# Layer 1 feed-forward: fetched expert results are added at another pace, from eight buffers instead of four

## The reference, cut to what matters

```python
x += sum over k of weight[t, k] * expert[e(t, k)](row[t])     # K = 4 of 32 experts, width 176
x += sigmoid(row @ w_shared_gate) * shared(row)                # width 704
shared(row) = (silu(row @ sw_gate) * (row @ sw_up)) @ sw_down
```

## Time and profile before

| what | us |
|---|---|
| median of 3 runs | 1801.31 |
| lowest and highest | 1800.06, 1802.41 |
| the profiled execution's own time | 1804.75 |
| its span, first to last instruction | 1802.7 |
| the end of layer 1's feed-forward, first shared down matmul to the last | 799.5 to 921.9 |
| the end of layer 2's feed-forward, to the closed statistics | 1348.6 to 1402.8 |

### The profile page before, as it was taken

One profiled execution on the slowest core, in us unless ns is written; L12 is line 12 of the kernel. 1 busy time (PEld: TensorE's weight loads), 2 busy tenths in 40 slices (PEclk: granted clock), 3 DMA queues, 4 the chain that ended last, 5 costly groups with the idle time before them and its releaser, 6 DMA issues. The chain is left out here.

```text
span 1802.7 us, 30396 instructions
## 1 busy us (share of the span) xinstructions
PE 1430.4 (79%) x8275; PEld 909.8 (50%) x8291; DVE 1149.8 (64%) x2546; ACT 754.5 (42%) x2273; POOL 595.2 (33%) x576
## 2 busy tenths in 40 slices
PE   4999993567589588997779999876883699975994
PEld 2565651345444253763346666553651466653552
DVE  3788887788578775324448999844335688844224
ACT  2766663344420032320027777521320588831321
POOL 2111100778477214335611111013436101002662
PEclk9999997898899678998879999957997799966997
DMA  7000000000010120962210001212433100411224
GB/s 251 10 6 9 9 4 1 1 0 0 13 35 0 52 91 29 305 213 80 87 31 10 12 9 62 87 56 56 122 102 87 36 24 23 154 52 33 82 81 154
DMA packets 73877, 111.35 MB, mean 62 GB/s; under 512 B 10381, under 2 KB 53200, under 8 KB 73296
## 3 DMA queue, kind: packets, MB, share of 16 engines
q1 hardware_dynamic: 61520, 77.99, 13.1%
q0 software_dynamic: 12288, 32.53, 6.5%
HBM read 87.41 MB, written 24.12 MB: 62 GB/s over the span
## 5 line engine op out<-in xcount | busy, mean ns | idle before, releaser
L523 ACT ACTIVATE l0a_prob<-l0a_ps_s,l0a_neg_max 128x128 f32<-128x128 f32 x512 | 141.0, 422 | 77.8 <-DVE l0a_neg_max L398 77.8
L523 ACT ACTIVATE l2a_prob<-l2a_ps_s,l2a_neg_max 128x128 f32<-128x128 f32 x512 | 141.0, 425 | 55.4 <-DVE l2a_neg_max L398 55.4
L878 ACT ACTIVATE l3a_prob<-l3a_ps_s,l3a_neg_max 128x256 f32<-128x256 f32 x256 | 104.5, 482 | 30.6 <-DVE l3a_neg_max L801 29.2
L398 DVE TENSOR_REDUCE l0a_neg_max<-l0a_ps_s 128x4 f32<-128x512 f32 x128 | 81.9, 684 | 38.0 <-PE l0a_ps_s L616 37.9
L369 POOL TENSOR_TENSOR l2a_k_head<-l2a_kT,head_of_row 128x512 f32<-128x512 f32 x32 | 32.6, 1041 | 178.7 <-ACT l2a_kT L504 178.7
L398 DVE TENSOR_REDUCE l2a_neg_max<-l2a_ps_s 128x4 f32<-128x512 f32 x128 | 82.1, 683 | 13.5 <-PE l2a_ps_s L616 13.4
L801 DVE TENSOR_REDUCE l3a_neg_max<-l3a_ps_s 128x2 f32<-128x512 f32 x128 | 84.2, 682 | 8.3 <-PE l3a_ps_s L929 8.0
L178 POOL TENSOR_TENSOR ln_rstd<-ln_var_eps,minus_half 128x16 f32<-128x16 f32 x8 | 23.4, 2921 | 196.3 <-POOLq L149 130.4
L1515 PE MATMUL l1a_ps_y<-l1a_kv,l1a_tap 128*128 128x512 f32 x192 | 84.2, 601 | 3.7 <-POOL l1a_kv L1487 3.7
L406 DVE COPY l2a_probT<-l2a_ps_t 128x512 f32<-128x512 f32 x128 | 82.0, 682 | 4.7 <-PE l2a_ps_t L625 4.6
L406 DVE COPY l0a_probT<-l0a_ps_t 128x512 f32<-128x512 f32 x128 | 82.1, 684 | 3.2 <-PE l0a_ps_t L625 3.1
(11 more groups left out here) (453 smaller groups left out, 3645.8 us busy)
## 6 DMA issues: line engine op xcount, KB each, us to landing
l1f_w_gu<-in_l1f_w_gu SPq DMA_DIRECT2D x32, 352.0 KB
expert_results<-l2f_y_sb SPq DMA_DIRECT2D x48, 128.0 KB
l1f_w_d<-in_l1f_w_d SPq DMA_DIRECT2D x32, 176.0 KB
expert_results<-l1f_y_sb SPq DMA_DIRECT2D x32, 128.0 KB
l2f_w_gu_all<-in_l2f_w_gu SPq DMA_DIRECT2D x1, 4096.0 KB, 13.7
l3f_w_gu_all<-in_l3f_w_gu SPq DMA_DIRECT2D x1, 4096.0 KB, 15.2
l3f_got<-expert_results SPq DMA_DIRECT2D x16, 256.0 KB, 5.1
x_rows<-in_x SPq DMA_DIRECT2D x8, 256.0 KB, 4.7
```

Of the source, the lines that this page charges most:

```text
L398: dve.tensor_reduce(neg_max[:, j, :], ps_s[j][:, :].rearrange("p (r k) -> p r k", r=R), AX.X, ALU.max, negate=True).then_inc(max_done, 1)
L523: last = act.activation(prob[4 * c + j][:, r * P:r * P + P], ps_s[j][:, r * P:r * P + P], ACT.Exp, bias=neg_max[:, j, r:r + 1])
L878: last = act.activation(prob[4 * c + j][:, m * D:m * D + D], ps_s[j][:, m * D:m * D + D], ACT.Exp, bias=neg_max[:, j, m:m + 1])
```

## The change

POOL gets eight `got` buffers instead of four in layer 1 (NG = GOT where `capacity` is set, which is layer 1 alone), with eight semaphores, and so may fetch eight tiles ahead of DVE's additions. And a tile is added per K * 768 columns instead of K * 640: 3072 instead of 2560 in layer 1, and, since the line is shared, 1536 instead of 1280 in layer 2. Layer 3 has no shared part and does not use the count.

```diff
-        self.gathered = [ctx.enter_context(nc.semaphore(f"gathered{r}")) for r in range(RING)]
+        self.gathered = [ctx.enter_context(nc.semaphore(f"gathered{r}")) for r in range(GOT)]
...
-    NG = GOT if push else RING
+    NG = GOT if push or capacity else RING
...
-                if t >= RING:
-                    pool.wait_ge(added, t - (RING - 1))
+                if t >= NG:
+                    pool.wait_ge(added, t - (NG - 1))
                 for k in range(K):
                     pool.indirect_dma_start(
-                        out=got[t % RING][:, k, :], out_offset=None, in_=results,
+                        out=got[t % NG][:, k, :], out_offset=None, in_=results,
                         in_offset=bass.IndirectOffsetOnAxis(ap=from_slot[:, t, k:k + 1], axis=0))\
-                        .then_inc(got_in[t % RING], 16)
+                        .then_inc(got_in[t % NG], 16)
...
-                add_results(max(with_results, min(B, columns // (K * 640) - 1)))
+                add_results(max(with_results, min(B, columns // (K * 768) - 1)))
```

More of the change, by code:

```diff
@@ L109, in __init__ @@
         self.xin_in = [ctx.enter_context(nc.semaphore(f"xin_in{r}")) for r in range(RING)]
-        self.gathered = [ctx.enter_context(nc.semaphore(f"gathered{r}")) for r in range(RING)]
+        self.gathered = [ctx.enter_context(nc.semaphore(f"gathered{r}")) for r in range(GOT)]
         self.result_out = [ctx.enter_context(nc.semaphore(f"result_out{r}")) for r in range(RING)]
-        self.n_xin_in, self.n_gathered = 0, 0
+        self.n_xin_in, self.n_gathered = 0, [0] * GOT
         self.conv_in = ctx.enter_context(nc.semaphore("conv_in"))
@@ L1668, in moe_ffn @@
         y_out = [sem(f"y_out{r}") for r in range(RING)]
-        xin_in, got_in = core.xin_in, core.gathered
+        xin_in = core.xin_in
         if push:
-            got_in, y_out = [sem(f"got_in{r}") for r in range(NG)], core.result_out
-        xin_before, got_before = core.n_xin_in, core.n_gathered
+            y_out = core.result_out
+        xin_before, got_before = core.n_xin_in, tuple(core.n_gathered)
         core.n_xin_in += NT // RING * 16
-        core.n_gathered += B // RING * K * 16
+        got_in = [sem(f"got_in{r}") for r in range(NG)] if push else core.gathered[0:NG]
+        if not push:
+            for r in range(NG):
+                core.n_gathered[r] += B // NG * K * 16
         n_loads = 1 + rms + biased
@@ L2072, in add_results @@
                 for t in range(with_results, until):
-                    dve.wait_ge(got_in[t % NG], (t // NG + 1) * 16 if push else got_before + (t // NG + 1) * 16 * K)
+                    dve.wait_ge(got_in[t % NG], (t // NG + 1) * 16 if push else got_before[t % NG] + (t // NG + 1) * 16 * K)
                     for k in range(K):
```

## The result

The changed kernel takes 1809.84 us (median of 5 runs, 1806.38 to 1814.7); the kernel before took 1801.54 beside it (5 runs, 1800.06 to 1803.0). The ratio is 1.0047, with a 95% interval of 1.0031 to 1.0063: 8.3 us slower.

The account below looks back on a forecast made before the run. It took PE, held up in layer 1's end by its semaphores arriving late beside long gather runs, as the bound. 4.8 + 13.6 - 7.5 + 0 = +10.9 us gave a median of 1812, range 1800 to 1822.

Parts of the forecast that it names:

- a step 15 before 841: Layer 1's end: sign that PE's signals pass during the long gather run, which would make the prediction wrong.
- the rule on which the second term rests: After gathers run unbroken some 12 to 17 us, PE's signals are held until the run is over; +13.6 us rested on it.
- The tail: Layer 1's end: fetched tiles 14 and 15 follow the last shared tile, delaying the closing of the statistics: +4.8 us.
- The first run: Layer 1's end: 36 gathers instead of 24, so PE restarts at 850.6 instead of 837.0: +13.6 us.
- held to the end of the run: Layer 1: signals of steps 13 and 14 come at 849.2, the gather run's end plus 2.3 us.
- the bound of zero: Layer 1's first gather run: no loss if step 13's signal passes at 835.6 and step 14's with it.
- rival 3: Faster: the hold has its own length, signal at 835.6, both later holes vanish; -10.1 us, 1791, chance 0.14.
- The later runs: Layer 1's later gathers: two holes with slow restarts, 14.9 us, give way to one of 7.4: -7.5 us.
- Layer 2: Layer 2's end: its run of 16 gathers is cut into 10 and 6; 0, between -1.5 and +2.5 us.
- 1 (no later hold): Layer 1's end: breaks in POOL's pace suffice to prevent later holds; +3.5 us, 1805, chance 0.17.
- rival 2: Lateness has nothing to do with gathers and stays at the same places, only the tail: +4.8 us, 1806, chance 0.08.
- rival 4: Worse: all later holes stay as long as now and layer 2 pays 2.5 us; +20.9 us, 1822, chance 0.11.

Follow-up runs that it names:

- the second comparison: Kernel before and changed kernel rerun, plus gathers cut by pauses or replaced by clearing, on a chip with late signals; kernel before 1802.99 us.
- after_again: The changed kernel once more, unchanged, against the kernel before: 1812.52 us, ratio 1.0057.
- pace_only: Kernel before with only the new count (3072 columns instead of 2560), four buffers kept: 1777.22 us, ratio 1.0027.
- before_again: The kernel before once more, unchanged, for its trace: 1801.69 us.
- eight_only: Changed kernel with the old count (2560), so eight buffers alone, against the kernel before: 1772.06 us, ratio 0.9996; repeats 1772.49 and 1773.08.
- memset_again: Kernel before with each layer 1 gather replaced by POOL clearing the same buffer, expert results left out, late-signal chip: 1770.99 us, one execution.
- the first comparison: Each half of the change, two buffers, and layer 1's gathers replaced by clearing, each against the kernel before, which took 1772.63 us there.
- third and fourth: Two comparisons of eight buffers alone and of short breaks with the new count, against the kernel before at 1771.65 and 1773.0 us.
- memset_for_gather: Kernel before with each layer 1 gather replaced by POOL clearing the same buffer, expert results left out, chip without late signals: 1770.9 us, one execution.
- pause2_4us: Kernel before with POOL clearing an unused weight buffer six times after each 8 gathers of layer 1: 1822.57 us, ratio 1.0113.
- pause_short: Kernel before with the new count and one clearing of a used buffer after each 8 layer 1 gathers: 1789.84 us, ratio 1.0099; repeat 1788.04, 1.0077.

## Why the prediction was right, and where it was not

The forecast was +10.9 on the profiled execution, 1812 for the median. Measured were +8.3 (1809.84) and, in the second comparison, +9.5 (1812.52). In the stretch alone, for which the prediction's terms sum to +10.9, the two pairs of profiles give +6.9 and 131.38 - 118.08 = +13.3. The same kernel's stretch differs by some 5 us between two profiled executions (123.58 and 118.08), so a sum of holes is no better than that. The time lies in the range, and the change is slower, as forecast. But one of the signs that the prediction itself set for being wrong, "a step 15 before 841", did come: step 15 began at 835.14. The tail and the later part were right in kind; the rule on which the second term rests was not, and that its size came out right, in the pair of the result, is luck.

1. **The tail**, +4.8. Measured 6.46 - 1.17 = +5.3, and 6.45 in after_again and pace_only. The missing half microsecond is mainly the 0.44 us of idle in the middle of tile 14's addition (at 925.23). Right.

2. **The first run**, +13.6. The step that failed is "held to the end of the run": step 13's signal was to come at 849.2, 2.3 us behind a run of 36, and step 15 to begin at 850.6. Instead the signal came at 833.77 in the middle of the run, 15.6 us late but at nearly the same place as before (835.62), and step 15 began at 835.14. That the signal had come behind the end of the run of 24 in the earlier trace rows looks like a coincidence, by the four distances of 31 to 34 us from the run's start. So tile 1 was added during the run, tile 9's gathers joined it, and the run became 40. Step 14's signal then was held to its end, and step 16 had to wait until 856.14, where it had begun at 842.82 before: +13.3. Two errors cancelled: four gathers more made the run 5.0 us longer than forecast, and the wait met one step later, a step that had taken 5.8 us before (837.00 to 842.82). I had named the bound of zero, "nothing if a signal slips through at 835.6 as before and step 14's with it"; step 13's came through and step 14's did not. In the second pair step 16 begins 17.5 us later, counted from the start of the stretch (57.65 us behind it in after_again, 40.12 in before_again), so the size met the 13.6 in one pair of two. The first half of rival 3, that the signal comes at 835.6 whatever POOL does, was right for step 13.

3. **The later runs**, -7.5, with one hole of 7.4 left, of 3 to 8 us between 865 and 885. Too gloomy: one hole of 1.13 us was left, at 885.13, in after_again one of 1.21, with the four matmuls behind it at 1.98 us in both. From the start of step 16 to PE's end were 79.0 us before and 67.0 after, -12.0. In the second pair it is 76.75 and 67.25, -9.5. What is left of the late signals there costs little, since the runs are 4 and 12 gathers long.

4. **Layer 2**, 0 between -1.5 and +2.5. Measured -1.65. The run of 16 was cut into 10 and 6 as expected (then 4 and 18, where 16 had followed), and the hold was spared. The end of layer 2, 51.08 us, is as long as in pace_only on a chip without late signals (51.14). There the same break costs 2.5 us against eight_only's 48.6. So the -1.65 is the spared hold less the price of the break.

By points 1 to 3 the stretch is 5.3 + 13.3 - 12.0 = +6.6, against the measured +6.9; the 0.3 is that the stretch itself began 0.32 us earlier (799.17 against 799.49). In the second pair the sum is 5.3 + 17.5 - 9.5 = +13.3, as measured. Of the rivals, 1 (no later hold) had the mechanism of the later part right, but its 1805 lies 4.8 us below the median, the forecast 2.2 above; rival 2 is refuted by memset_again; of rival 3 the faster end did not come, because of the hole of 15.46 us ahead of step 16; rival 4 is refuted by point 3.

What the prediction could not see is its condition. On chips 0, 15 and 5 the kernel before runs at 1771.65 to 1773.0, and there no trace has a late signal at all. By eight_only and pace_only the change would then be worth the tail and the break in layer 2, +4.6 us by pace_only's median, and the terms 2 and 3 nothing; the whole change did not run there, so this is an estimate. The late signals are about all of the 29 us between the two kinds of chip: the stretch is 123.58 against eight_only's 95.24, and the end of layer 2 52.73 against 48.6.

**The rule that I weighed.** On the chip with late signals the matmuls keep their pace beside the gathers, 1.88 us for four, and yet the kernel is 30.7 us shorter without them. On the chip of the first comparison taking them out is worth 1.7 us, by one execution. The Trainium skill's page "SBUF — State Buffer", section "Who interferes with whom", has DMA never contending with a compute engine. By that rule memset_again would have been no quicker. So the runs agree with it on the first chip, as far as one execution tells, and not on the second. What was late is the signal, not the matmul's access to memory, of which the page speaks, so the page may be right in its words and still mislead here.

**What stays open.** Whether the making of the gathers' descriptors or the movement of their data holds the signals; a kernel with plain transfers in their place was not run. What lets one signal through in a long run and holds the next. Whether eight buffers alone are a loss where signals are late: eight_only met three chips without them, so that the long run costs 13.3 or 17.5 us there is read from two pairs of traces, and not isolated by a run. And why one chip has late signals and another not: the result and the second comparison have them, with the kernel before at 1801.54 and 1802.99, the first, third and fourth have not. One more thing goes with it. The view of the DMA issues gives the time to landing of layer 2's gathers (in the last place of the line) in all eight traces of chips 0, 15 and 5 and in none of the six others, in which updates of the transfers' semaphores are missing (before's trace holds 6153, pace_only's, with the same transfers, 9008). Here memset_again, then memset_for_gather, one program on two chips:

```profile
l2f_got<-expert_results,l2f_from_slot POOLq DMA_INDIRECT x32
l2f_got<-expert_results,l2f_from_slot POOLq DMA_INDIRECT x32, 2.7
```

So the two kinds of trace differ in the gathers' own updates too. What that means is not shown.

## What to carry to other kernels

When a trace shows an engine waiting with the release "remote" for work that had long ended, lay the timelines of all other engines beside it and look for what ends just before the release; that found here what no busy share tells. Buffers added so that transfers run further ahead are worth nothing when nobody waits for the transfers (the view of the fetched tile said so), and they change when the transfers go out, which can cost. Take a gain or loss of half a per cent to more than one chip before tuning for it: here the same kernel differs by 1.7% between comparisons, which is more than any edit of its buffers. And when a signal comes just behind the end of something, look in a second trace whether it moves with that end; here one did and one did not.

## What the runs showed of the hardware

- In the result's traces and on chip 1, TensorE's semaphores came up to 29 us late (step 14: 28.9 in after, 25.0 in after_again) while POOL issued indirect gathers (128 rows of 1 KB, one per 1.25 us) in runs of 12 to 40. The first signal still held when a run ended came 0.1 to 4.0 us behind its end. On chips 0, 15 and 5, 64 gathers in a row delayed nothing. The kernel before takes 1801.5 to 1803.0 us with late signals and 1771.7 to 1773.0 without.
- A signal can come in the middle of such a run (821.62 in the earlier trace rows, 819.06 and 833.77 after), itself 3.5 to 15.6 us late, while the next is held. Step 13's came 31 to 34 us behind the run's start with 24 gathers and with 40.
- With runs of eight gathers and breaks of 7 to 9 us no signal was late in the stage, though the same execution had one late behind a run of 16 in layer 2.
- In before, after and their repeats, after PE had stood idle for 4.1 to 15.6 us, its next four matmuls of a step took 3.6 to 3.8 us instead of 1.88, at a granted clock of 0.50 to 0.56 where I read it; after 1.1 to 1.5 us of idle they took 1.98.
- POOL's clearing of 128x704 took 0.70 us, but with a drain behind it and gathers around it POOL then stood idle for up to 3.4 us in pause2_4us and 4.1 in pause_short.
